# Score matmuls whose contraction rows are packed as 128, 128 and 33, the 33-row ones of two query blocks in different halves of the array

## The chip, the cores and the metric

The kernel runs on one core of one Trainium2 chip. The metric is the time of one execution on the device in microseconds (us), as the median of several runs. Everything read from a trace comes from one profiled execution.

## What is computed

A decoder layer for 16 batches of 100 rows of width 128, with a context of 1444 rows of width 96 a batch. All is float32.

```python
x = x + self_attention(layernorm(x), wq, wk, wv)          # one head, rope, causal
x = x + cross_attention(layernorm(x), ctx, Wq, Wk, Wv, Wo, bo)
x = x + (quantized(layernorm(x)) @ (ternary - 1).T + bias)

# cross_attention: 16 heads of 64
scores = einsum('bqhd,bkhd->bhqk', q, k) / 8              # 16 * 100 queries x 1444 keys a batch
attn = softmax(scores)
out = einsum('bhqk,bkhd->bqhd', attn, v) @ Wo + bo
```

## The kernel before

**Folded weights.** The kernel never forms keys and values by head. At the start it computes, for each head, M = Wq Wk^T (128 x 96) and G = Wv Wo (96 x 128), in *m_bank* and *g_bank*, with 64 contraction rows a head. A batch's queries times M give *q*, 96 rows by 1600 columns (16 heads x 100 queries). The scores are then q against the context itself, transposed (*cT*, 96 rows by keys).

**Split operands.** The matrix unit takes operands rounded to a shorter form (F32R). To keep precision each operand is split into a rounded part and the rest: q_hi and q_lo, cT_hi and cT_lo, and the exponentials pr_hi and pr_lo, the context cN_hi and cN_lo. A product takes three matmuls: hi x hi, hi x lo, lo x hi. For the scores that is 97 + 96 + 96 contraction rows; the 97th is a row of ones in cT_hi and the negated row maximum (*negmax*) in q_hi, so that the maximum is subtracted inside the matmul.

**Steps.** A batch has 24 steps: 2 pairs of query blocks (800 queries each) by 12 chunks of 128 keys. A step's scores are 6 matmuls of 400 columns, three terms by two blocks *a*, each block into its own PSUM bank (*scores*, L1075). ScalarE takes the exponential of both banks twice (L610 in float32, L613 rounded, to *pr* and *pr_hi*), VectorE forms *pr_lo* (L879), and two steps later come the values, 6 matmuls of 400 columns with 128 contraction rows (*values*, L1107, or 2 in L1091 for the last chunk). The output of a pair is copied to *o_sb* (L575).

**Everything else** goes into slots between those matmuls, by a table written by hand (*AT*: step, what, for which batch). The items take turns in two PSUM banks; TensorE's *fill* writes one when VectorE's *consume* has freed it (semaphores misc_ready and misc_free). They are: the self-attention of the batch after next (T1, QK, V, S, PT, AO, T2), the next batch's q (in steps 0, 3, 5 and 8; ScalarE's *high_q*, L568, rounds it, VectorE's L658 forms q_lo), its row maxima (*max*, 39 matmuls of 482 columns in L929, reduced by VectorE in L663, up to four a step), their transpose (*negmax*, step 21), and the rest of the batch before (y, T3, F). In the last batch *sums* (L974, 16 matmul rows of one contraction row each, at partition 96) and *yh* (L979) take the place of *y* (L967). VectorE works its items of a step off, then waits for the exponentials and forms pr_lo.

**POOL** forms cT_lo (L488, L492) and cN_lo (L498) of the next batch and normalizes the output (L505, L506). **The SP queue** issues all DMAs in program order: for a batch the sums of the batch before (move_sums), then, when the splits of the next batch are done (split_done), the context of the batch after it (load_ctx), the store of the batch before, and the negmax row of the next batch (move_negmax: two DMAs from negmaxT into row 96 of q_hi, L391 and L393). The scores of a batch wait for that row and for cT_lo (L1062, L1063). In batch 0 the first part of the row is a DMA of its own (L410). q_hi, q_lo, cT_hi and cT_lo have two buffers each, one for every other batch.

The 12 batches in the middle are a loop of 6 turns with two batches each.

Of the kernel before, what the change touches and what calls it, by code (L numbers as in the profile page):

```python
# [35 lines left out]
def decoder_layer(nc, x_in, ctx_in, ctx_last_in, ctxT_in, wself_in, wqT_in, wkT_in, wvT_in, wo_in, bo_in,  # L36
# [6 lines left out]
    DH, H, _ = wqT_in.shape  # L43
# [25 lines left out]
    LOOPED = B - 4  # L69
    assert STEPS % RING == 0 and STEPS % 2 == 0 and Q % PAIR == 0 and BLK <= 512  # L70
# [3 lines left out]
    with ExitStack() as stack:  # L74
# [14 lines left out]
        wqT = sb("wqT", [DH, H, D])  # L89
        wkT = sb("wkT", [DH, H, DC])  # L90
        wvT = sb("wvT", [DH, H, DC])
        wo = sb("wo", [DH, H, D])
# [34 lines left out]
        o_sb = sb("o_sb", [DC + 1, Q])  # L127
        rrow = sb("rrow", [1, Q])
        rball = sb("rball", [DC, Q])
# [40 lines left out]
        ctx_in_s = sem("ctx_in_s")  # L170
        row_a_in_s = sem("row_a_in_s")
# [182 lines left out]
        def _(sp):  # L354
# [30 lines left out]

            def move_negmax(n, par, use, first=0):


                sp.wait_ge(misc_free, use + 1)
                full = Q // P  # L390
                sp.dma_start(q_hi[par][DC:DC + 1, first * P:full * P].bitcast(F32),  # L391
                             negmaxT[0:full - first, :].bitcast(F32)).then_inc(row_in_s, 16)
                sp.dma_start(q_hi[par][DC:DC + 1, full * P:Q].bitcast(F32),  # L393
                             negmaxT[full - first:QT - first, P - (Q - full * P):P].bitcast(F32)).then_inc(row_in_s, 16)
# [37 lines left out]
        NCONST = 4 + 2 * 6  # L432
# [3 lines left out]
        def _(pool):  # L436
# [19 lines left out]
            def padding(i):  # L456

                constant(cT_hi[i][:, NT:NCH * P], 0.0)
                constant(cT_lo[i][:, NT:NCH * P], 0.0)
                constant(cN_hi[i][:, FULL, :], 0.0)  # L460
                constant(cT_hi[i][DC:DC + 1, 0:NT], 1.0)
# [22 lines left out]
            def split_T(n, par, rows_in=0):  # L484
                pool.wait_ge(cThi_done, 2 * (n + 1))
                at_least(pool, st_ready, (n - 1) * STEPS)
                half = NT // 2
                nc.gpsimd.tensor_tensor(out=cT_lo[par][:, 0:half], in0=cT_raw[:, 0:half],  # L488
                                        in1=cT_hi[par][0:DC, 0:half].bitcast(F32), op=ALU.subtract)

                at_least(pool, rrow_in_s, rows_in * 16)
                nc.gpsimd.tensor_tensor(out=cT_lo[par][:, half:NT], in0=cT_raw[:, half:NT],  # L492
                                        in1=cT_hi[par][0:DC, half:NT].bitcast(F32), op=ALU.subtract).then_inc(cTlo_done, 1)
# [7 lines left out]
            def normalize(n):  # L501
# [3 lines left out]
                order.link(nc.gpsimd.partition_broadcast(rball[:, :], rrow[:, :]))  # L505
                nc.gpsimd.tensor_tensor(out=o_sb[0:DC, :], in0=o_sb[0:DC, :], in1=rball[:, :],  # L506
# [41 lines left out]
        def _(act):  # L548
# [17 lines left out]
            def high_q(n, par, j, use, bank):  # L566
                act.wait_ge(misc_ready, use + 1)
                nc.scalar.activation(q_hi[par][0:DC, j * BLK:(j + 1) * BLK], banks[0:DC, bank, 0:BLK],  # L568
                                     ACT.Copy).then_inc(qhi_done, 1)

            def evacuate(n, pair, y_use=None):
# [3 lines left out]
                nc.scalar.activation(o_sb[:, pair * PAIR:(pair + 1) * PAIR].rearrange("p (a q) -> p a q", a=2),  # L575
# [615 lines left out]
```

## Time and profile before

| what | value |
|---|---|
| median of 3 runs | 1241.41 us (1240.72 to 1242.85) |
| span of the profiled execution | 1241.1 us |
| TensorE matmul rows busy | 1159.2 us, 93% |
| weight loads busy | 1047.9 us, 84% |
| VectorE busy | 1005.4 us, 81% |
| ScalarE busy | 691.1 us, 56% |
| GpSimd (POOL) busy | 245.7 us, 20% |
| mean granted TensorE clock | 0.981 of full |

The profiled execution has a span of 1241.1 us, 0.3 us less than the median of the runs. A batch takes about 74 us, a step about 3.0. Matmuls are pipelined, so the rows of two that follow each other overlap, and a busy share says little of how densely they are issued; the distance between two starts says it. PEld rows are weight loads; each matmul has one.

### The profile page before, as it was taken

What the parts mean: (1) busy time and instruction counts of PE and PEld (TensorE: products, weight loads), DVE (VectorE), ACT (ScalarE), POOL (GpSimd) and SP (SyncE); (2) the same over time, 40 slices, a digit from 0 to 9 for tenths busy, and PEclk for the clock granted to TensorE, in tenths of its full rate; (3) what the DMA queues carried; (4) which work ended last, traced back from release to release, by engine and by line L of the source; (5) the groups of instructions that cost most, each with busy time, mean ns of one, the idle gap of its engine ahead of it and who ended that gap; (6) DMA issues with size and microseconds to landing.
All of it is one profiled execution on the core that took longest, in us unless ns stands there. A gap on an engine that the chain in (4) does not pass through costs nothing.

```text
span 1241.1 us, 20286 instructions
## 1 busy us (share of the span) xinstructions
PE 1159.2 (93%) x6561; PEld 1047.9 (84%) x6561; DVE 1005.4 (81%) x1625; ACT 691.1 (56%) x969; POOL 245.7 (20%) x228
## 2 busy tenths in 40 slices
PE   7789999999999999999999999999999999999997
PEld 5568889898898888888898888989889898988996
DVE  2698888988788798887979878898788889888655
ACT  1245656556464665656556554655556466564653
POOL 3120130302213022130302213130221303022010
PEclk9799999999899999999999999999999999999997
DMA  6101010010101001010000101001010100100000
GB/s 143 38 1 39 1 39 3 6 36 2 39 3 39 4 2 38 4 38 5 16 25 1 39 4 38 3 1 41 3 39 3 39 2 2 40 2 1 3 1 4
DMA packets 12727, 24.40 MB, mean 20 GB/s; under 512 B 4934, under 2 KB 8654, under 8 KB 12494
## 3 DMA queue, kind: packets, MB, share of 16 engines
q1 hardware_dynamic: 12622, 23.00, 6.9%
q8 instruction: 65, 1.06, 0.4%
q14 instruction: 40, 0.33, 0.1%
HBM read 21.88 MB, written 0.82 MB: 18 GB/s over the span
## 4 chain that ended last, share of the span: by engine, by line
PE 77%; issue 10%; DVE 10%; ACT 1%; DMA 1%; DVEq 1%; POOL 0%; SPq 0%; POOLq 0%; ACTq 0%
PE banks L1075 27%; PE banks L1107 26%; PE banks L929 9%; PE banks L967 4%; PE banks L920 4%; DVE pr_lo L879 3%; DVE maxes L663 3%; PE banks L949 1%; DVE cN_hi L775 1%; ACT pr_hi L613 1%; DMA q_hi<-negmaxT 1%; PE banks L1091 1%; PE banks L1010 1%; PE banks L960 1%; PE banks L1038 1%
## 5 line engine op out<-in xcount | busy, mean ns | idle before, releaser
L610 ACT ACTIVATE pr<-banks 128x800 f32<-128x800 f32 x384 | 322.4, 840 | 442.4 <-PE banks L1075 438.3
L879 DVE TENSOR_TENSOR pr_lo<-pr,pr_hi 128x800 fp32r<-128x800 f32 x352 | 424.0, 1205 | 61.2 <-ACT pr_hi L613 54.1
L663 DVE TENSOR_REDUCE maxes<-banks 128x1 f32<-128x482 f32 x585 | 372.5, 653 | 51.0 <-PE banks L929 45.9
L613 ACT ACTIVATE pr_hi<-banks 128x800 fp32r<-128x800 f32 x384 | 319.1, 831 | 0.0
L929 PE MATMUL banks<-cT_hi,q_hi 96*128 96x482 f32 x585 | 228.4, 390 | 27.5 <-DVE maxes L663 18.1
L1075 PE MATMUL banks<-q_hi,cT_hi 97*128 97x400 f32 x768 | 215.6, 362 | 9.1 <-DMA q_hi<-negmaxT 6.9
L1075 PE MATMUL banks<-q_hi,cT_lo 96*128 96x400 f32 x768 | 208.5, 352 | 0.0
L1075 PE MATMUL banks<-q_lo,cT_hi 96*128 96x400 f32 x768 | 203.9, 346 | 0.0
L1107 PE MATMUL banks<-pr_hi,cN_hi 128*97 128x400 f32 x704 | 187.7, 348 | 0.0
L1107 PE MATMUL banks<-pr_lo,cN_hi 128*97 128x400 f32 x704 | 186.9, 347 | 0.6 <-DVE pr_lo L879 0.6
L1107 PE MATMUL banks<-pr_hi,cN_lo 128*96 128x400 f32 x704 | 186.3, 346 | 0.0
L1075 PEld LDWEIGHTS banks<-q_hi,cT_hi 97*128 97x128 f32 x768 | 135.2, 191 | 20.6 <-ACT pr_hi L613 6.4
L929 PEld LDWEIGHTS banks<-cT_hi,q_hi 96*128 96x128 f32 x585 | 109.9, 188 | 50.3 <-DVE maxes L663 26.2
L1075 PEld LDWEIGHTS banks<-q_lo,cT_hi 96*128 96x128 f32 x768 | 143.2, 190 | 0.0
L1075 PEld LDWEIGHTS banks<-q_hi,cT_lo 96*128 96x128 f32 x768 | 139.2, 190 | 3.3
L475 POOL TENSOR_TENSOR ve<-mv,eps 100x1 f32<-100x1 f32 x48 | 9.2, 192 | 616.6 <-DVE mv L642 616.6
L1107 PEld LDWEIGHTS banks<-pr_lo,cN_hi 128*97 128x97 f32 x704 | 115.0, 164 | 16.5 <-DVE pr_lo L879 1.1
L1107 PEld LDWEIGHTS banks<-pr_hi,cN_lo 128*96 128x96 f32 x704 | 114.5, 163 | 15.9
L1107 PEld LDWEIGHTS banks<-pr_hi,cN_hi 128*97 128x97 f32 x704 | 114.3, 164 | 12.5
L506 POOL TENSOR_TENSOR o_sb<-o_sb,rball 96x1600 f32<-96x1600 f32 x15 | 55.6, 3706 | 105.8 <-issue 105.8
L920 PEld LDWEIGHTS banks<-x2T,M 128*96 128x96 f32 x512 | 56.8, 175 | 7.6 <-DVE maxes L663 1.4
L920 PE MATMUL banks<-x2T,M 128*96 128x100 f32 x512 | 59.6, 263 | 2.2 <-DVE maxes L663 1.1
(117 smaller groups left out, 888.3 us busy)
## 6 DMA issues: line engine op xcount, KB each, us to landing
cT_raw<-in_ctxT SPq DMA_DIRECT2D x16, 568.5 KB
cN_raw<-in_ctx SPq DMA_DIRECT2D x16, 528.0 KB
out<-result SPq DMA_DIRECT2D x16, 50.0 KB
X<-in_x SPq DMA_DIRECT2D x1, 700.0 KB
cN_raw<-in_ctx_last SPq DMA_DIRECT2D x16, 40.5 KB
wqT<-in_wqT SPq DMA_DIRECT2D x1, 512.0 KB, 5.4
wo<-in_wo SPq DMA_DIRECT2D x1, 512.0 KB, 13.3
wkT<-in_wkT SPq DMA_DIRECT2D x1, 384.0 KB, 7.0
```

The costliest lines, as they stand in the source:

```text
L506: nc.gpsimd.tensor_tensor(out=o_sb[0:DC, :], in0=o_sb[0:DC, :], in1=rball[:, :], op=ALU.mult).then_inc(on_done, 1)
L610: nc.scalar.activation(pr[:, s % 2, :].rearrange("p (a q) -> p a q", a=2), pair, ACT.Exp, scale=float(DH) ** -0.5).then_inc(exp_done, 1)
L613: nc.scalar.activation(pr_hi[:, s % RING, :].rearrange("p (a q) -> p a q", a=2), pair, ACT.Exp, scale=float(DH) ** -0.5).then_inc(hi_done, 1)
L663: nc.vector.tensor_reduce(maxes[:, t, p:p + 1], here[:, 0:PW], AX.X, ALU.max).then_inc(misc_free, 1)
L775: nc.vector.scalar_tensor_tensor(out=cN_hi[par][0:ROWS, FULL, 0:DC], in0=last_hi[:, :].bitcast(F32), scalar=last[0:ROWS, 0:1], in1=cN_raw[ ...
L879: nc.vector.tensor_tensor(low[rows, s % RING, :], pr[rows, s % 2, :], pr_hi[rows, s % RING, :].bitcast(F32), ALU.subtract).then_inc(lo_don ...
L920: mm = nc.tensor.matmul(here[0:DC, i * S:(i + 1) * S], M[:, h, :], x2T[par][:, :], start=True, stop=True)
L929: mm = nc.tensor.matmul(here[:, 0:PW], q_hi[par][0:DC, qtile(t):qtile(t) + P], cT_hi[par][0:DC, PAT[p]:PAT[p] + PW], start=True, stop=True)
L949: mm = nc.tensor.matmul(here[:, m * S:(m + 1) * S], wself[:, m, :], xnT[par][:, :], start=True, stop=True)
L967: mm = nc.tensor.matmul(here[0:S, 0:D], o_sb[0:DC, h * S:(h + 1) * S], G[:, h, :], start=(h == 0), stop=(h == H - 1))
L1075: mm = nc.tensor.matmul(banks[:, ST + 2 * (s % 2) + a, 0:BLK], k, q[:, q0:q0 + BLK], start=(i == 0), stop=(i == 2))
L1107: mm = nc.tensor.matmul(banks[0:m, OUT + a, 0:BLK], k, e[:, r, a * BLK:(a + 1) * BLK], start=False, stop=(s % NCH == NCH - 1 and i == 2))
```

## The change

The 289 contraction rows of the scores, 97 + 96 + 96, are packed anew, as 128 + 128 + 33:

- a: q_a holds q_hi (96 rows) and q_lo's rows 64 to 95 at partitions 96 to 127; cT_a holds cT_hi (96 rows) and again cT_hi's rows 64 to 95.
- b: q_b holds q_lo's rows 0 to 63 and q_hi's rows 0 to 63; cT_b holds cT_hi's rows 0 to 63 and cT_lo's rows 0 to 63.
- c: q_c holds q_hi's rows 64 to 95 and the negmax row, 33 rows, and the same again at partitions 64 to 96; cT_c holds cT_lo's rows 64 to 95 and the row of ones, also twice.

A step's six score matmuls become two with a, two with b, two with c. The c matmul of block 0 uses partitions 0 to 32, that of block 1 partitions 64 to 96, each into its own bank as before. The number of matmuls, their columns and all sums are the same.

The copies between partitions are made by new DMAs in the SP queue: five for cT (move_c, 224 rows of 1516 words a batch) and three for q (move_q, 128 rows of 1600 words a batch). The negmax row goes out twice, in four DMAs. cT_lo has one buffer now. VectorE forms q_lo in two instructions (32 rows and 64 rows) instead of one. The weights of M and G are stored as 8 heads in partitions 0 to 63 and 8 heads in partitions 64 to 127, and wkT and wvT lie in buffers that are used only later. The maxima (L929) use q_a and cT_a, with 96 rows as before.

```diff
-        q_hi = two("q_hi", [DC + 1, Q], F32R)
-        q_lo = two("q_lo", [DC, Q], F32R)
-        cT_hi = two("cT_hi", [DC + 1, NCH * P], F32R)
-        cT_lo = two("cT_lo", [DC, NCH * P], F32R)
+        q_a = two("q_a", [P, Q], F32R)
+        q_b = two("q_b", [P, Q], F32R)
+        q_c = two("q_c", [HALF + TOP + 1, Q], F32R)
+        cT_a = two("cT_a", [P, NCH * P], F32R)
+        cT_b = two("cT_b", [P, NCH * P], F32R)
+        cT_c = two("cT_c", [HALF + TOP + 1, NCH * P], F32R)
+        cT_lo = sb("cT_lo", [DC, NT], F32R)
...
+            def move_c(n, par):
+
+                sp.wait_ge(cThi_done, 2 * (n + 1))
+                sp.dma_start(cT_a[par][DC:P, 0:NT].bitcast(F32),
+                             cT_a[par][HALF:DC, 0:NT].bitcast(F32)).then_inc(cdup_in_s, 16)
+                sp.dma_start(cT_b[par][0:HALF, 0:NT].bitcast(F32),
+                             cT_a[par][0:HALF, 0:NT].bitcast(F32)).then_inc(cdup_in_s, 16)
+                sp.wait_ge(cTlo_done, n + 1)
+                sp.dma_start(cT_b[par][HALF:P, 0:NT].bitcast(F32), cT_lo[0:HALF, :].bitcast(F32)).then_inc(cdup_in_s, 16)
+                for half in (0, HALF):
+                    sp.dma_start(cT_c[par][half:half + TOP, 0:NT].bitcast(F32),
+                                 cT_lo[HALF:DC, :].bitcast(F32)).then_inc(cdup_in_s, 16)
+
+            def move_q(n, par):
+
+                sp.wait_ge(qhi_done, QB * (n + 1))
+                sp.dma_start(q_b[par][HALF:P, :].bitcast(F32), q_a[par][0:HALF, :].bitcast(F32)).then_inc(qdup_in_s, 16)
+                for half in (0, HALF):
+                    sp.dma_start(q_c[par][half:half + TOP, :].bitcast(F32),
+                                 q_a[par][HALF:DC, :].bitcast(F32)).then_inc(qdup_in_s, 16)
...
+                for row in (TOP, HALF + TOP):
+                    sp.dma_start(q_c[par][row:row + 1, first * P:full * P].bitcast(F32),
+                                 negmaxT[0:full - first, :].bitcast(F32)).then_inc(row_in_s, 16)
+                    sp.dma_start(q_c[par][row:row + 1, full * P:Q].bitcast(F32),
+                                 negmaxT[full - first:QT - first, P - (Q - full * P):P].bitcast(F32)).then_inc(row_in_s, 16)
...
+            move_c(0, 0)
             split_done(0)
             load_ctx(1)
+            move_q(0, 0)
             sp.wait_ge(misc_free, NSTART)
-            sp.dma_start(q_hi[0][DC:DC + 1, 0:FIRST * P].bitcast(F32),
-                         negmaxT[0:FIRST, :].bitcast(F32)).then_inc(row_a_in_s, 16)
+            for row in (TOP, HALF + TOP):
+                sp.dma_start(q_c[0][row:row + 1, 0:FIRST * P].bitcast(F32),
+                             negmaxT[0:FIRST, :].bitcast(F32)).then_inc(row_a_in_s, 16)
...
                     move_sums(b - 1)
+                if present(b, 1):
+                    move_c(b + 1, 1 - par)
                 if present(b, 2):
                     split_done(b + 1)
                     load_ctx(ahead)
+                if present(b, 1):
+                    move_q(b + 1, 1 - par)
...
-                    nc.vector.tensor_tensor(q_lo[par][:, j * BLK:(j + 1) * BLK], here[0:DC, 0:BLK],
-                                            q_hi[par][0:DC, j * BLK:(j + 1) * BLK].bitcast(F32),
-                                            ALU.subtract).then_inc(misc_free, 1)
+                    cols = slice(j * BLK, (j + 1) * BLK)
+                    nc.vector.tensor_tensor(q_a[par][DC:P, cols], here[HALF:DC, 0:BLK],
+                                            q_a[par][HALF:DC, cols].bitcast(F32), ALU.subtract)
+                    nc.vector.tensor_tensor(q_b[par][0:HALF, cols], here[0:HALF, 0:BLK],
+                                            q_a[par][0:HALF, cols].bitcast(F32), ALU.subtract).then_inc(misc_free, 1)
...
-                terms = [(cT_hi[par][0:DC + 1, keys], q_hi[par][0:DC + 1, :]),
-                         (cT_hi[par][0:DC, keys], q_lo[par][:, :]),
-                         (cT_lo[par][:, keys], q_hi[par][0:DC, :])]
-                k, q = terms[i]
                 for a in range(2):
+                    rest = slice(a * HALF, a * HALF + TOP + 1)
+                    terms = [(cT_a[par][:, keys], q_a[par][:, :]), (cT_b[par][:, keys], q_b[par][:, :]),
+                             (cT_c[par][rest, keys], q_c[par][rest, :])]
+                    k, q = terms[i]
                     q0 = pair * PAIR + a * BLK
                     mm = nc.tensor.matmul(banks[:, ST + 2 * (s % 2) + a, 0:BLK], k, q[:, q0:q0 + BLK],
                                           start=(i == 0), stop=(i == 2))
```

Here P is 128, DC 96, HALF 64 and TOP 32. The scores of a batch wait for all copies (cdup_in_s, qdup_in_s) and for the four row DMAs.

## Rows read from the trace of the kernel before

**Rows 1.** The page's header and part 1: busy us (share of span) xinstructions.
```profile
span 1241.1 us, 20286 instructions
...
PE 1159.2 (93%) x6561; PEld 1047.9 (84%) x6561; DVE 1005.4 (81%) x1625; ACT 691.1 (56%) x969; POOL 245.7 (20%) x228
```

**Rows 2.** The page's part 4, the chain that ended last, by engine.
```profile
PE 77%; issue 10%; DVE 10%; ACT 1%; DMA 1%; DVEq 1%; POOL 0%; SPq 0%; POOLq 0%; ACTq 0%
```

**Rows 3.** The same chain in order of time, in the middle: start, us, what.
```profile
570.27 1.10 PE banks L1075 x6
571.36 1.09 PE banks L1107 x6
```

**Rows 4.** Waits of TensorE: line, released by, us in total, times, longest.
```profile
PE banks L929 <- DVE maxes L663: 18.1, 21, 3.1
PE banks L960 <- DVE maxes L663: 15.2, 13, 2.8
...
PE banks L929 <- DVE V L700: 7.5, 14, 0.6
```

**Rows 5.** Timeline, steady stream: start, us, engine, line, operation, rows*columns, moving operand.
```profile
627.33 0.35 PE L1075 MATMUL banks<-q_lo,cT_hi 96*128 96x400 f32 x1
627.33 0.37 PEld L1075 LDWEIGHTS banks<-q_hi,cT_lo 96*128 96x128 f32 x2
```

**Rows 6.** Timeline, last batch, into the one-row matmuls.
```profile
1204.34 0.34 PE L1107 MATMUL banks<-pr_lo,cN_hi 128*97 128x400 f32 x1
1204.61 0.25 PEld L974 LDWEIGHTS banks<-cT_hi,o_sb 1*100 1x100 f32 x2 [0.28 <-issue]
```

**Rows 7.** Timeline, the end, out of the one-row matmuls.
```profile
1228.33 0.22 PE L974 MATMUL banks<-cT_hi,o_sb 1*100 1x1 f32 x1
1228.48 0.54 PEld L979 LDWEIGHTS banks<-G,o_sb 96*100 96x100 f32 x3
```

**Rows 8.** Timeline, the start: out of the 64-row matmuls.
```profile
28.54 0.41 PE L1010 MATMUL banks<-wo,wvT 64*96 64x128 f32 x1
28.88 0.56 PEld L920 LDWEIGHTS banks<-x2T,M 128*96 128x96 f32 x3 [0.28 <-issue]
```

**Rows 9.** Timeline, last batch, the first full-height pair behind the one-row matmuls.
```profile
1206.11 0.30 PEld L1075 LDWEIGHTS banks<-q_hi,cT_hi 97*128 97x128 f32 x2
1206.58 0.35 PE L1075 MATMUL banks<-q_lo,cT_hi 96*128 96x400 f32 x1
```

**Rows 10.** POOL and TensorE near 320; L775 everywhere (ns, min/median/max).
```profile
317.80 3.02 POOL L498 TENSOR_TENSOR cN_lo<-cN_raw,cN_hi 128x1056 fp32r<-128x1056 f32 x1
...
321.55 0.75 PE L960 MATMUL banks<-V,prT 100*100 100x128 f32 x2 [2.82 <-DVE maxes L663]
...
L775 DVE SCALAR_TENSOR_TENSOR cN_hi<-last_hi,last,cN_raw x16: 304/308/2306, 49.5 to 1126.6; 108x96 fp32r<-108x96 f32 x16
```

**Rows 11.** VectorE's groups by shape: xcount, busy us, mean ns, idle before and releaser.
```profile
L879 DVE TENSOR_TENSOR pr_lo<-pr,pr_hi 128x800 fp32r<-128x800 f32 x352 | 424.0, 1205 | 61.2 <-ACT pr_hi L613 54.1 <-issue 3.9 <-ACT pr L610 1.8
L663 DVE TENSOR_REDUCE maxes<-banks 128x1 f32<-128x482 f32 x585 | 372.5, 653 | 51.0 <-PE banks L929 45.9
L658 DVE TENSOR_TENSOR q_lo<-banks,q_hi 96x400 fp32r<-96x400 f32 x64 | 35.1, 548 | 10.6 <-ACT q_hi L568 9.4
```

**Rows 12.** Timeline: the SP queue's last issue and the next batch's first score matmul.
```profile
132.25 0.56 SPq L393 DMA_DIRECT2D q_hi<-negmaxT  x1
...
135.29 0.53 PE L1075 MATMUL banks<-q_hi,cT_hi 97*128 97x400 f32 x2
```

**Rows 13.** SP issues, first scores; a window (last: granted clock, DMA share, GB/s).
```profile
50.75 0.40 SPq L367 DMA_DIRECT2D cN_raw<-in_ctx_last  x1
54.70 0.89 SPq L410 DMA_DIRECT2D q_hi<-negmaxT  x1
...
56.91 0.67 PE L1075 MATMUL banks<-q_hi,cT_hi 97*128 97x400 f32 x1 [2.55 <-DMA q_hi<-negmaxT]
...
321.90:325.30 3.40, 3.40 (x12) 2.95 (x12) 2.82 (x6) 1.56 (x2) 0.00 (x0) 0.50 0.87 245
```

More of the change, by code:

```diff
@@ L69, in decoder_layer @@
     LOOPED = B - 4
+    HALF = P // 2
+    TOP = DC - HALF
+    assert DC + TOP == P and TOP == 32
     assert STEPS % RING == 0 and STEPS % 2 == 0 and Q % PAIR == 0 and BLK <= 512
@@ L567, in high_q @@
                 act.wait_ge(misc_ready, use + 1)
-                nc.scalar.activation(q_hi[par][0:DC, j * BLK:(j + 1) * BLK], banks[0:DC, bank, 0:BLK],
+                nc.scalar.activation(q_a[par][0:DC, j * BLK:(j + 1) * BLK], banks[0:DC, bank, 0:BLK],
                                      ACT.Copy).then_inc(qhi_done, 1)
@@ L928, in fill @@
                         pe.wait_ge(qhi_done, n * QB + bank_of[t] + 1)
-                    mm = nc.tensor.matmul(here[:, 0:PW], q_hi[par][0:DC, qtile(t):qtile(t) + P],
-                                          cT_hi[par][0:DC, PAT[p]:PAT[p] + PW], start=True, stop=True)
+                    mm = nc.tensor.matmul(here[:, 0:PW], q_a[par][0:DC, qtile(t):qtile(t) + P],
+                                          cT_a[par][0:DC, PAT[p]:PAT[p] + PW], start=True, stop=True)
                 elif what == "max_b":
                     t, p = divmod(j, PIECES)
-                    mm = nc.tensor.matmul(here[:, 0:PW], q_hi[par][0:DC, qtile(t):qtile(t) + P],
-                                          cT_hi[par][0:DC, PAT[p]:PAT[p] + PW], start=True, stop=True)
+                    mm = nc.tensor.matmul(here[:, 0:PW], q_a[par][0:DC, qtile(t):qtile(t) + P],
+                                          cT_a[par][0:DC, PAT[p]:PAT[p] + PW], start=True, stop=True)
                 elif what == "negmax_a":
@@ L974, in fill @@
                         mm = nc.tensor.matmul(here[0:S, i:i + 1], o_sb[DC:DC + 1, q0:q0 + S],
-                                              cT_hi[par][DC:DC + 1, 0:1].bitcast(F32), start=True, stop=True)
+                                              cT_c[par][DC:DC + 1, 0:1].bitcast(F32), start=True, stop=True)
                 elif what == "yh":
@@ L996, in start, with head @@
                     fill(n, n, what, 0, k, MISC + k % 2, behind)
+            def head(h):
+                first = h // (H // 2) * DH
+                return slice(first, first + DH), h % (H // 2)
             def m_bank(j):
                 for i in range(4):
-                    mm = nc.tensor.matmul(banks[:, j, i * DC:(i + 1) * DC], wqT[:, 4 * j + i, :],
-                                          wkT[:, 4 * j + i, :], start=True, stop=True)
+                    rows, h = head(4 * j + i)
+                    mm = nc.tensor.matmul(banks[:, j, i * DC:(i + 1) * DC], wqT[rows, h, :], wkT[rows, h, :],
+                                          start=True, stop=True)
                 mm.then_inc(mg_ready, 1)
@@ L1009, in g_bank @@
                 for i in range(4):
-                    mm = nc.tensor.matmul(banks[0:DC, GBANKS[j], i * D:(i + 1) * D], wvT[:, 4 * j + i, :],
-                                          wo[:, 4 * j + i, :], start=True, stop=True)
+                    rows, h = head(4 * j + i)
+                    mm = nc.tensor.matmul(banks[0:DC, GBANKS[j], i * D:(i + 1) * D], wvT[rows, h, :], wo[rows, h, :],
+                                          start=True, stop=True)
                 mm.then_inc(mg_ready, 1)
@@ L1037, in _ @@
                 for p in range(PIECES):
-                    mm = nc.tensor.matmul(banks[:, PIECES * (t % 2) + p, 0:PW], q_hi[0][0:DC, qtile(t):qtile(t) + P],
-                                          cT_hi[0][0:DC, PAT[p]:PAT[p] + PW], start=True, stop=True)
+                    mm = nc.tensor.matmul(banks[:, PIECES * (t % 2) + p, 0:PW], q_a[0][0:DC, qtile(t):qtile(t) + P],
+                                          cT_a[0][0:DC, PAT[p]:PAT[p] + PW], start=True, stop=True)
                 mm.then_inc(max0_ready, 1)
@@ L1167, with halves @@
     cos, sin = np.cos(ang).astype(np.float32), np.sin(ang).astype(np.float32)
+    def halves(w):
+        return w.reshape(DH, 2, H // 2, w.shape[2]).transpose(1, 0, 2, 3).reshape(2 * DH, H // 2, w.shape[2])
     def by_head(w):
-        return np.asarray(w).reshape(w.shape[0], H, DH).transpose(2, 1, 0)
+        return halves(np.asarray(w).reshape(w.shape[0], H, DH).transpose(2, 1, 0))
     named = {
```

62 lines of the change are left out of this document (31 added, 31 removed).

## The prediction

> **What bounds the kernel now.** I read the header and the busy line of the page first [rows 1]. TensorE's matmul rows cover 93% of the span, VectorE 81%, ScalarE 56%. The busy share of TensorE can't be trusted alone, since its rows overlap: one 400-column matmul is shown as 0.35 us long, but its successor starts 0.18 us later. So I went on to the chain that ended last. It lies on TensorE for 77% of the span and on VectorE for 10% [rows 2], and in order of time it reads six score matmuls in 1.10 us, six value matmuls in 1.09 us, again and again [rows 3]. That is 0.183 us for a matmul, whether it contracts 96, 97 or 128 rows. VectorE enters the chain where TensorE has to wait for it: 18.1 us and 7.5 us ahead of the maxima (L929) and 15.2 us ahead of L960, 41 us in these three [rows 4]. What a wait of the queue adds before and after is not in those numbers. So the kernel is bound by the issue of matmuls, with short stops where VectorE has fallen behind: what the change does to the time between two matmuls counts nearly whole, 384 times (16 batches of 24 steps).
>
> **The six score matmuls of a step.** Their number stays six: two of 128 rows, two of 128 rows, and two of 33, at partitions 0 and 64. Rows cost nothing, as said, so the first four keep 4 x 0.183 us. All that can change is the last pair. Two things may happen to it: the two may run at the same time, and the array may have to be regrouped from 128 rows to halves of 64 and back, since everything before and behind the pair uses more than 64 rows.
>
> The trace of before has such regroupings, outside the steady loop, and they are not free. In the steady stream the weights of the next matmul load as soon as the running one starts: the matmul starts at 627.33, and so does the load of the next one, 627.33 [rows 5]. In the last batch the "sums" matmuls contract one row, at partition 96. The last full-height matmul before them starts at 1204.34, is 0.34 long, and the first weight load of the one-row group comes at 1204.61, 0.27 us after that start instead of 0.00 [rows 6]. That load waited for nothing that the profile shows ("issue"). The way back is the same: the last one-row matmul starts at 1228.33, is 0.22 long, and the load of the 96-row one comes at 1228.48 [rows 7]. In both the load begins 0.07 us before the shown end of the last matmul of the other height: it waits until the array has run empty. With 64-row matmuls it is seen too, at the start of the kernel, where all matmuls take longer: the last one starts at 28.54, the load of the 128-row one behind it at 28.88 [rows 8]. Between 96, 97 and 128 rows there is no such gap: the two lines follow each other at 0.183 [rows 3].
>
> Behind each gap the weights are no longer hidden. After the gap the load starts at 1206.11; the two matmuls of its pair are followed by the next line at 1206.58, so the first of them really began at 1206.58 - 2 x 0.183 = 1206.21, 0.10 us after its load. The second load of the pair starts 0.30 - 0.19 = 0.11 us after the first [rows 9].
>
> So a step goes like this, from the start of the last 128-row score matmul: 0.27 until the first 33-row load, 0.11 until the second, 0.10 until the second 33-row matmul runs (the first has started 0.11 earlier and they overlap), 0.27 until the load of the next full-height one, 0.10 until that runs: 0.85 us. Before it was 3 x 0.183 = 0.55 us. That is +0.30 us a step, 384 x 0.30 = +115 us.
>
> The bounds of this: if the second 33-row matmul doesn't overlap the first but follows at 0.183, the step costs 0.075 more, 384 x 0.375 = +144 us. If nothing is drained and the two overlap fully but for the second load (0.11 + 0.11 - 0.183, so 0.03 late), the pair takes one matmul's time: -0.15, and 384 x -0.15 = -58 us. The row nearest to the case is the one of the kernel itself at full clock, the drain, and I take +0.30 for it; that two halves overlap is shown by no row here, and I take it because the weight loads of one group already overlap a running matmul.
>
> The Trainium skill, "TensorEngine Tiling (Array Packing)", Key Properties, says that a change of the tiling mode, not just of the tile, drains TensorE. By that rule the sum is the one above, and the rows agree with it: 0.27 us in place of 0.00. The skill's "TensorE: Matmul & The Clock Gate", Part 3, gives the span of packed tiles as one matmul and some 4 ns for each further tile; alone it would give the -58 us, or 384 x -0.18 = -69 us. It speaks of a stream that stays packed, and here two of twelve matmuls are.
>
> **What VectorE gives back.** TensorE stands still for 41 us behind VectorE [rows 4], and every such stop also leaves the next weights unhidden, 0.1 us for each of the 48 in these three rows, 5 us. VectorE's work, 1005 us, doesn't shrink; a step of TensorE that is 0.3 us longer lets it catch up. One step with three maxima costs VectorE 1.2 + 3 x 0.65 = 3.2 us [rows 11] and TensorE 12 x 0.183 for the 400 columns and 3 x 0.183 x 482 / 400 for the maxima, 2.9 us, with the change 3.2. So most of these stops go. I take 40 us back of the 46 (bounds 15 and 60, below). Some batches have a worse stop: POOL's L498, 3.02 us long, runs when VectorE comes to L775, which takes up to 2.31 us where 0.31 is its median, and TensorE stops for 2.8 us [rows 10]. Right behind it the granted clock is 0.50, the 1.2 GHz level, for all of a window of 3.4 us [rows 13], which costs about half of that again, 1.7 us. Longer steps move POOL and VectorE against each other. If no batch meets it any more, the clock comes back too, and 60 us return; if many do, only 15.
>
> **Smaller terms.** *q_lo* is now written in two pieces. One piece of 96 rows and 400 columns takes 0.55 us [rows 11]. If the time goes with the columns, the second piece costs that again, 64 x 0.55 = 35 us of VectorE's own time; if it went with the rows, nothing. Both pieces have the 400 columns, so I take the 35. It has the room (1040 of over 1300 us), but in the steps 0, 3, 5 and 8 it holds back maxima behind it: I charge 6 us, between 0 and 35.
>
> The *maxima row* goes out in four DMAs instead of two. The SP queue issues the last of the two at 132.25; the first matmul that needs it is at 135.29 [rows 12], and TensorE doesn't wait there. The landing time is known from the start: issued at 54.70, waited for until 56.91 [rows 13], so 2.2 us. The slack is 135.29 - 132.25 - 2.2 = 0.8 us, and the last of four is issued two issues later, 0.56 + 0.89 = 1.4 us; but two longer steps lie between, +0.6. So 0.0 us a batch in my case, 1.4 + 0.3 - 0.8 = 0.9 where steps get shorter (15 batches, 14 us).
>
> The *copies* of move_c (224 rows of 1516 words, 1.36 MB) and of move_q (128 rows of 1600, 0.82 MB) stand in the same SP queue. In a batch they have tens of us. At the start they don't: move_q is queued behind load_ctx(1), whose 1.14 MB (568.5, 528.0 and 40.5 KB) are issued up to 51.15, and the first scores, at 56.91, come to wait for both [rows 13]. At the 245 GB/s of the stretch with the densest transfers, loads and copies take 1.96 MB / 245 GB/s = 8.0 us; from 50 on, with the 2.2 us until something lands, that is some 60.5, so +4 us, with the rows of the maxima behind it in the queue (bounds 0 and 8). In batch 0 the second part of the maxima row is 1.4 us later too; its cover is unknown, +1. POOL's two more memsets for each buffer stand ahead of nothing that is late. The weights M and G are computed by the same number of matmuls from halves of 64 rows that all lie in one half per bank: nothing.
>
> **Sum.** 1241.1 (span of the profiled execution; with 0.3 around it the median of the runs, 1241.4) + 115 + 6 + 0 + 4 + 1 - 40 = 1327, and 0.3 around it: **1328 us**.
>
> **The rivals.**
> *A (forecast, 0.72)*: drained twice a step. Own range: with 60 us given back 1308, and with the 6 and 5 us of small terms hidden as well 1297; high with no overlap of the halves (+29) at 1357: 1296 to 1357.
> *B, drained once a step (0.10)*: only the regrouping into halves waits, and the full-height load behind the pair is started as usual. 0.27 + 0.11 + 0.10 + 0.18 = 0.66 against 0.55: 384 x 0.11 = +42 us, + 11 small terms, - 20 given back: 1274. For it: a load into other rows might be allowed. Against it: the ways back [rows 7, 8].
> *C, the other side (0.11)*: no drain, the halves run together. -58, + 5 at the start, + 14 for the maxima row, + 6, and 15 more of waits for VectorE, whose 3.2 us in a step with three maxima are then the longer: 1223. For it: the rows that show a drain are few, and all of them are of operands declared F32, where the scores have F32R ones. Against it: in [rows 6] the matmul before the gap is an F32R one, and F32 matmuls of 96 rows follow F32R ones without a gap. It decides from the point where a regrouping costs less than half of the 0.15 us won, 0.075; the rows show 0.19 (0.27 + 0.10 - 0.18).
> *D, the change does nothing (0.07)*: neither drained nor overlapped, the pair takes 2 x 0.183 as ever. What is left are the small terms, 1241 + 11 = 1252, to 1246 if the start is covered.
>
> **How the numbers follow.** The predicted time is A's. The range leaves out C and the tails: 1246 to 1357 holds about 0.67 of A, all of B, and most of D, some 0.8. Faster by over 0.2% (about what a measurement of this kernel can tell from no change) is C: 0.11. Within 0.2% is the lower edge of D: 0.02. Slower is the rest, 0.87.
>
> **What would show it.** In the profile after: each step has two gaps in the weight loads, 0.27 us after the last 128-row score matmul and 0.27 us after the second 33-row one; the two 33-row matmuls start about 0.11 us apart; six scores and the way back take 1.40 us in place of 1.10. The waits of L929 and L960 for VectorE are a third of what they were. The first scores start near 60 or 61 us. If the loads of the 33-row pair stand directly at the start of the matmul before them, C or D is right, and the distance between the two 33-row matmuls tells which. I'd be wrong with the right mechanism if the halves don't overlap, or if POOL and VectorE now collide in many batches.

## The result: slower by 3.8%

The changed kernel takes 1289.39 us (median of 4, 1286.28 to 1291.63) where the kernel before, on the same chip, takes 1241.58 (median of 4, 1240.72 to 1242.85). The ratio is 1.0376, with a 95% interval of 1.035 to 1.0403: 48 us more. The forecast was 1328, +87, with 1246 to 1357 as its range. So the side was right and the mechanism too, as the following shows, but the forecast change was nearly double the measured one.

The page of the profiled execution after (1286.3 us, span 1284.5), the lines that answer to [rows 1] and [rows 2], and the two groups of the new 33-row matmuls:

```profile
span 1284.5 us, 20543 instructions
...
PE 1226.5 (95%) x6561; PEld 955.0 (74%) x6561; DVE 1022.2 (80%) x1689; ACT 692.0 (54%) x969; POOL 245.6 (19%) x232
...
PE 81%; DVE 9%; issue 7%; ACT 1%; DMA 1%; DVEq 1%; POOL 0%; SPq 0%; POOLq 0%; ACTq 0%
...
L1123 PE MATMUL banks<-q_c,cT_c 33*128 33x400 f32 x768 | 173.3, 447 | 0.0
...
L1123 PEld LDWEIGHTS banks<-q_c,cT_c 33*128 33x128 f32 x768 | 71.8, 184 | 98.3 <-issue 93.1
```

The same 6561 matmuls fill 67 us more, and the weight loads 93 us less than in [rows 1]: two loads of each step now lie over each other, which is 384 x 0.19 = 73 of the 93. The last number pair of the last row is what to see: the load engine was idle for 98.3 us ahead of the 33-row loads, 93.1 of it with nothing that the profile shows as a reason. Spread over 384 steps that is 0.26 us a step, the 0.27 of [rows 6].

One step on TensorE in the timeline after, in the middle of the kernel, answering to [rows 3] and [rows 5]:

```profile
632.44 0.53 PE L1123 MATMUL banks<-q_b,cT_b 128*128 128x400 f32 x2
632.90 0.19 PEld L1123 LDWEIGHTS banks<-q_c,cT_c 33*128 33x128 f32 x2 [0.26 <-issue]
632.90 0.45 PE L1123 MATMUL banks<-q_c,cT_c 33*128 33x400 f32 x2
633.28 0.19 PEld L969 LDWEIGHTS banks<-cT_a,q_a 96*128 96x128 f32 x1 [0.19 <-issue]
633.28 0.48 PE L969 MATMUL banks<-cT_a,q_a 96*128 96x482 f32 x1
633.60 0.34 PE L1155 MATMUL banks<-pr_hi,cN_hi 128*97 128x400 f32 x1
```

The second b matmul starts at 632.44 + 0.18 = 632.62. The 33-row loads come 0.28 us after it. A row with x2 covers both instructions: the two loads take 0.19 us together, where [rows 9] had 0.30 for a pair, and the two matmuls 0.45, as long as one of them alone (mean 447 ns above). So both start at the same time: over all 384 pairs the second starts 0.002 to 0.004 us after the first, loads and matmuls alike. The next full-height load comes 0.38 us after them. The value matmul at 633.60 is behind the maxima's 482 columns, 0.22 us, so the maxima really began at 633.38. From the last full-height start to the next it is 0.76 us, where three matmuls took 0.55: +0.21 us a step, and 384 x 0.21 = 81 us.

TensorE's waits after (line, released by, us in total, times, longest), answering to [rows 4]:

```profile
PE banks L969 <- DVE maxes L703: 13.3, 17, 1.7
PE banks L969 <- DVE q_b L699: 6.2, 8, 1.1
...
PE banks L1123 <- DMA q_c<-q_a: 5.8, 1, 5.8
...
PE banks L1000 <- DVE maxes L703: 2.1, 6, 0.7
PE banks L1123 <- DMA q_c<-negmaxT: 1.9, 2, 1.0
```

L969 and L1000 are the lines L929 and L960 of before. The two waits for maxima, 18.1 and 15.2 us, have become 13.3 and 2.1, and the wait for V has gone from 7.5 to 0.6. The wait for q_b, 6.2, was one of 1.6 for q_lo before. Together that is 42.4 before and 22.2 after. The rows of the maxima are waited for 1.9 us in all, in spite of the four DMAs. The 5.8 us are the start:

```profile
60.42 1.01 PE L1123 MATMUL banks<-q_a,cT_a 128*128 128x400 f32 x2 [5.79 <-DMA q_c<-q_a]
...
65.00:70.00 5.00, 4.69 (x13) 3.09 (x13) 4.21 (x8) 2.06 (x3) 3.65 (x4) 0.50 0.00 0
70.00:75.00 5.00, 5.00 (x15) 3.80 (x14) 3.79 (x7) 1.56 (x2) 0.62 (x1) 0.50 0.00 0
```

The first scores start 3.5 us later than in [rows 13], and the granted clock stays at 0.50, the 1.2 GHz level, until 75.0. In the kernel before it is back at 61.2, 13.8 us earlier, and the window that follows has 1.00:

```profile
65.00:70.00 5.00, 2.89 (x17) 2.39 (x15) 4.99 (x7) 1.56 (x2) 2.15 (x2) 1.00 0.00 0
```

Over the whole kernel the mean clock is the same, 0.981 before and 0.982 after: what is lost at the start, before loses in later stretches (17 us at the 1.2 GHz level between 300 and 1200, where the changed kernel has none). The first exponential of batch 1 and that of batch 15 give the time of a batch between them, after and (second fence) before:

```profile
145.18 0.84 ACT L648 ACTIVATE pr<-banks 128x800 f32<-128x800 f32 x1 [0.98 <-PE banks L1123]
1204.48 0.84 ACT L648 ACTIVATE pr<-banks 128x800 f32<-128x800 f32 x1 [0.81 <-PE banks L1123]
```

```profile
136.67 0.84 ACT L610 ACTIVATE pr<-banks 128x800 f32<-128x800 f32 x1 [0.70 <-PE banks L1075]
1164.84 0.84 ACT L610 ACTIVATE pr<-banks 128x800 f32<-128x800 f32 x1 [0.62 <-PE banks L1075]
```

That is (1204.48 - 145.18) / 14 = 75.66 us a batch against 73.44: +2.2, where 24 steps of +0.21 would make +5.0. More than half of what the regrouping costs does not reach the end of a batch. Two questions stood, then: is the regrouping really the cause, and where does the other half go?

### The profile page after: what moved, and what is told of

Same layout as the page of the kernel before. It is cut to its first block, busy times and chain, and to the rows that moved or that the text cites. A ratio compares the mean times of both kernels' runs of the same rounds, so it can differ in the third digit from the quotient of the medians.

```text
span 1284.5 us, 20543 instructions
## 1 busy us (share of the span) xinstructions
PE 1226.5 (95%) x6561; PEld 955.0 (74%) x6561; DVE 1022.2 (80%) x1689; ACT 692.0 (54%) x969; POOL 245.6 (19%) x232
## 3 DMA queue, kind: packets, MB, share of 16 engines
q1 hardware_dynamic: 21454, 57.96, 18.1%
## 4 chain that ended last, share of the span: by engine, by line
PE 81%; DVE 9%; issue 7%; ACT 1%; DMA 1%; DVEq 1%; POOL 0%; SPq 0%; POOLq 0%; ACTq 0%
PE banks L1123 28%; PE banks L1155 28%; PE banks L969 12%; PE banks L1007 4%; PE banks L960 3%; DVE pr_lo L919 2%; DVE maxes L703 2%; PE banks L1139 1%; DVE q_a L697 1%; DVE q_b L699 1%; PE banks L989 1%; DMA q_c<-q_a 1%; PE banks L1000 1%; PE banks L1046 0%; DVE maxes L859 0%
## 5 line engine op out<-in xcount | busy, mean ns | idle before, releaser
L919 DVE TENSOR_TENSOR pr_lo<-pr,pr_hi 128x800 fp32r<-128x800 f32 x352 | 391.1, 1111 | 69.1 <-ACT pr_hi L651 64.8
L969 PE MATMUL banks<-cT_a,q_a 96*128 96x482 f32 x585 | 247.6, 423 | 20.4 <-DVE maxes L703 13.3
L1123 PE MATMUL banks<-q_a,cT_a 128*128 128x400 f32 x768 | 217.2, 364 | 9.2 <-DMA q_c<-q_a 5.8
L1123 PE MATMUL banks<-q_b,cT_b 128*128 128x400 f32 x768 | 203.7, 346 | 0.0
L1123 PE MATMUL banks<-q_c,cT_c 33*128 33x400 f32 x768 | 173.3, 447 | 0.0
L969 PEld LDWEIGHTS banks<-cT_a,q_a 96*128 96x128 f32 x585 | 109.8, 188 | 76.5 <-issue 28.0
L1123 PEld LDWEIGHTS banks<-q_a,cT_a 128*128 128x128 f32 x768 | 135.1, 192 | 22.8 <-issue 7.9
L1123 PEld LDWEIGHTS banks<-q_c,cT_c 33*128 33x128 f32 x768 | 71.8, 184 | 98.3 <-issue 93.1
L1123 PEld LDWEIGHTS banks<-q_b,cT_b 128*128 128x128 f32 x768 | 143.2, 189 | 0.0
L606 ACT ACTIVATE q_a<-banks 96x400 fp32r<-96x400 f32 x64 | 32.0, 501 | 60.9 <-PE banks L960 60.9
L960 PEld LDWEIGHTS banks<-x2T,M 128*96 128x96 f32 x512 | 55.8, 171 | 6.4 <-DVE maxes L703 1.2
```

The lines of the kernel that those rows point to most:

```text
L606: nc.scalar.activation(q_a[par][0:DC, j * BLK:(j + 1) * BLK], banks[0:DC, bank, 0:BLK], ACT.Copy).then_inc(qhi_done, 1)
L919: nc.vector.tensor_tensor(low[rows, s % RING, :], pr[rows, s % 2, :], pr_hi[rows, s % RING, :].bitcast(F32), ALU.subtract).then_inc(lo_don ...
L960: mm = nc.tensor.matmul(here[0:DC, i * S:(i + 1) * S], M[:, h, :], x2T[par][:, :], start=True, stop=True)
L969: mm = nc.tensor.matmul(here[:, 0:PW], q_a[par][0:DC, qtile(t):qtile(t) + P], cT_a[par][0:DC, PAT[p]:PAT[p] + PW], start=True, stop=True)
L1123: mm = nc.tensor.matmul(banks[:, ST + 2 * (s % 2) + a, 0:BLK], k, q[:, q0:q0 + BLK], start=(i == 0), stop=(i == 2))
```

## Experiments

All medians are in microseconds, and ratios are to the kernel before on the same chip (1241.1 to 1241.4 there).

**1. The 33-row matmuls at full height.** Everything of the change stays, but the c matmuls contract 97 rows (partitions 0 to 96, the unused ones zero), so that nothing is regrouped and nothing runs side by side. One copy to cT_c falls away with it.

```diff
-                    rest = slice(a * HALF, a * HALF + TOP + 1)
+                    rest = slice(0, HALF + TOP + 1)
```

> The changed kernel, but the c matmuls of both blocks are of full height (97 rows, partitions 0 to 96, the unused ones zero), so nothing is regrouped and nothing can overlap; copies, rows, q_lo in two pieces stay (one copy of eight is gone). Theory (the two regroupings of a step cost 0.42 us less the 0.21 that the overlap wins, 384 x 0.21 = 81 us, of which VectorE's waits had given back some 45): the step's scores take 1.10 us again, the waits for VectorE come back, and the time is near that of before plus the start, 1250 us (1244 to 1260). Rival (the time went to the new copies, the row DMAs and the second q_lo piece): it stays at 1285 to 1290.

1250.78 (1248.57 to 1255.13), ratio 1.0061 (1.0033 to 1.009). The six scores are back at 1.09 us, in the chain in order of time:

```profile
642.12 1.09 PE banks L1121 x6
```

So 38.6 of the 48 us come with the height of two matmuls in twelve, and 9.6 with everything else: the copies, the start and q_lo's two pieces. The chain says that a step lost its 0.21 us, 81 us in all; only 38.6 of them came off the time. A part of the others turned up as waits (L967 is L929 of before, L998 is L960):

```profile
PE banks L967 <- DVE maxes L701: 21.2, 20, 2.6
PE banks L998 <- DVE maxes L701: 8.7, 13, 0.7
PE banks L1121 <- DMA q_c<-negmaxT: 8.5, 12, 1.4
```

**2. Both 33-row matmuls in the same half.** Two regroupings a step as in the changed kernel, and no overlap.

```diff
-                    rest = slice(a * HALF, a * HALF + TOP + 1)
+                    rest = slice(0, TOP + 1)
```

> The changed kernel, but both 33-row matmuls use partitions 0 to 32, so they can't run at the same time; the regroupings stay. Theory: the second follows the first at 0.18 us instead of 0.003, 384 x 0.18 = +69 us, little of it given back since VectorE's stops are mostly gone: 1340 to 1360. Rival (the shown overlap is only in the records, the matmuls take turns anyway): no change, 1289.

1335.8 (1335.08 to 1341.19), ratio 1.0753 (1.0722 to 1.0784). The pair in the timeline:

```profile
641.43 0.29 PEld L1123 LDWEIGHTS banks<-q_c,cT_c 33*128 33x128 f32 x2
...
641.43 0.63 PE L1123 MATMUL banks<-q_c,cT_c 33*128 33x400 f32 x2
```

Now the pair of loads takes 0.29 and the pair of matmuls 0.63, instead of 0.19 and 0.45: in one half the second load comes 0.11 us after the first and the second matmul 0.18 behind. The overlap of the halves is real and worth 0.18 us a step, 69 us on TensorE, of which 46 show in the time. That is a little more given back than expected: 1335.8 lies under the 1340 to 1360. The prediction had charged the 0.11 us between the loads to the changed kernel. There they don't exist; they appear only here, in one half, and even here they cost nothing of their own: from the pair's loads to the next full-height load it is 0.56 us, the changed kernel's 0.38 and the second matmul's 0.18.

**3. One matmul more in each step of the kernel before.** The step gets longer by 0.183 us without any regrouping (the added product, cT_lo by q_lo for block 0, is also added to the scores).

```diff
+                if i == 1:
+                    q0 = pair * PAIR
+                    nc.tensor.matmul(banks[:, ST + 2 * (s % 2), 0:BLK], cT_lo[par][:, keys], q_lo[par][:, q0:q0 + BLK],
+                                     start=False, stop=False)
```

> The kernel before with one more matmul of 400 columns a step (the product of both low parts, added for block 0 alone): TensorE gets 384 x 0.183 = 70 us more work of a known size and nothing else changes. Theory (each 0.2 us that a step gets longer gives half of it back, since POOL's and VectorE's stops get out of the way): 1265 to 1290, and VectorE's long waits for POOL get fewer as in the changed kernel. Rival (what was given back came from something else in the change, the longer step counts whole): 1305 to 1312.

1281.63 (1277.01 to 1285.92), ratio 1.0307 (1.0271 to 1.0343): 40 of 384 x 0.183 = 70 us reach the end, 57%. Batches take 75.84 us. So time that is added to TensorE's step without any change of height is about half absorbed too. Waits are part of where it goes:

```profile
PE banks L929 <- DVE maxes L663: 14.5, 17, 1.9
PE banks L960 <- DVE maxes L663: 7.3, 13, 2.3
```

The other half of the expectation failed: VectorE's long pr_lo instructions did not get fewer (68 of over 1.2 us here, 64 in before), though in the changed kernel there are 39.

**4. The copies ahead of the next batch's context at the start.**

```diff
             move_c(0, 0)
+            move_q(0, 0)
             split_done(0)
             load_ctx(1)
-            move_q(0, 0)
```

> The changed kernel with batch 0's move_q ahead of split_done and load_ctx(1) in the SP queue. Theory (the first scores wait 5.8 us for the copies queued behind 1.14 MB, and that pause keeps the granted clock at half for 13.7 us longer, 6.8 us of work): first scores near 57, clock back at full near 60 us after the start of the records' pause, 1277 to 1282. Rival (the clock's return isn't tied to that pause): only the 3.5 us of the wait, 1285 to 1287.

1285.76 (1285.21 to 1289.41), ratio 1.0359 (1.0325 to 1.0394). That is the rival's time and not the theory's; it is 3.6 us under the changed kernel, and the ranges of the two overlap. The first scores come 2.2 us earlier, and the clock returns only 2 us earlier, at 72.9:

```profile
58.19 1.01 PE L1123 MATMUL banks<-q_a,cT_a 128*128 128x400 f32 x2 [3.25 <-issue]
...
70.00:75.00 5.00, 5.00 (x19) 3.91 (x20) 3.47 (x7) 3.02 (x4) 0.00 (x0) 0.71 0.00 0
```

The pause before the first scores became shorter by 2.5 us only, so this run doesn't separate it. Up to 90 us, the stretches at 0.50 are 44.2 to 61.2 in the kernel before; 41.8 to 65.7 and 69.1 to 72.5 in experiment 1, which has the long pause and no regrouping; 42.2 to 72.9 here; 44.3 to 75.0 in the changed kernel; 42.4 to 83.4 in experiment 2, whose regroupings have no overlap. With regroupings the clock returns later. But experiment 6, which has none, is at 0.50 from 42.3 to 66.2 and from 69.6 to 76.4, together as long as the changed kernel (30.7 us). So what keeps the clock low at the start stays open.

**5. q_lo in two pieces in the kernel before.** VectorE forms rows 64 to 95 and 0 to 63 by themselves, as the changed kernel does.

```diff
-                    nc.vector.tensor_tensor(q_lo[par][:, j * BLK:(j + 1) * BLK], here[0:DC, 0:BLK],
...
+                    nc.vector.tensor_tensor(q_lo[par][64:DC, cols], here[64:DC, 0:BLK],
...
+                    nc.vector.tensor_tensor(q_lo[par][0:64, cols], here[0:64, 0:BLK],
```

> The kernel before with q_lo formed in two VectorE instructions (rows 64 to 95 and rows 0 to 63) and nothing else. Theory (a part of the 9.7 us by which e1_full_height is over the kernel before is this second piece, 64 x 0.57 = 36 us of VectorE's time, hidden but for some holding back of maxima): VectorE's busy time up by 36, the run 2 to 8 us over before, 1243 to 1249. Rival (all of the 9.7 us is the start and its clock): 1241.

1243.65 (1241.79 to 1246.49), ratio 1.0011 (0.999 to 1.0033), not to be told from before. VectorE's own time rises by 21 us, not by 36. The two pieces take 37.8 us more than the one, but pr_lo gets shorter by 28.6 us and cN_hi (L775, [rows 10]) by 6.0, while *qk*, a sum in the self-attention that reads two tensors of SBUF, gets longer by 18.1 (first row: before; the others: this run):

```profile
L698 DVE TENSOR_TENSOR qk<-rt 128x200 f32<-128x200 f32 x16 | 5.9, 368 | 1.6
...
L881 DVE TENSOR_TENSOR pr_lo<-pr,pr_hi 128x800 fp32r<-128x800 f32 x352 | 395.4, 1123 | 60.2 <-ACT pr_hi L613 53.1 <-issue 2.8 <-ACT pr L610 1.8
...
L700 DVE TENSOR_TENSOR qk<-rt 128x200 f32<-128x200 f32 x16 | 24.0, 1501 | 1.6
```

pr_lo takes 1123 ns in the mean against 1205 [rows 11] and 1202 in experiment 3, where the steps are longer and q_lo is in one piece. Experiment 1, with two pieces and steps of the old length, has 1138, the changed kernel 1111. In these traces, one of each kernel, the shorter pr_lo thus goes with the two pieces of q_lo, which move VectorE against POOL, and not, as the forecast had it, with the longer steps. Nor does VectorE simply meet POOL less: qk takes 1.4 us in the changed kernel too, where it took 0.37 before. A part of the collisions has only moved to it.

**6. Five full-height matmuls a step.** Experiment 1 without the b matmul of block 1, which leaves that product out of the scores. A step then has the time that the packing would have if nothing were drained.

```diff
+                    if (i, a) == (1, 1):
+                        continue
```

> e1_full_height with the b matmul of block 1 left out (small parts of the product, not the maximum's row), so five full-height matmuls a step: TensorE's time as if the pair really cost one matmul and nothing were regrouped. Theory (per 0.18 us of a step about half reaches the end, from e3_one_more: 70 us more gave 40): 1250.8 - 35 = 1216, 1208 to 1228. Rival (VectorE and POOL hold the steps where they are once TensorE is faster): over 1235. Rival (TensorE bound alone, all of it counts): 1180.

1221.11 (1220.01 to 1226.03), ratio 0.9848 (0.9815 to 0.988): 30 us under experiment 1, of 70 taken off. TensorE now waits more, for VectorE and for the rows of the maxima:

```profile
PE banks L967 <- DVE maxes L701: 28.3, 28, 2.5
PE banks L967 <- DVE q_b L697: 15.8, 42, 1.0
PE banks L1123 <- DMA q_c<-negmaxT: 13.0, 9, 2.2
```

This is rival C, the undrained packing, as nearly as it can be run (it takes 70 us off TensorE where C had 58), and its 1223 was close.

**7. POOL's long instructions in pieces, in the kernel before.** The product of 1600 columns in four of 400, the forming of cN_lo in three.

```diff
-                nc.gpsimd.tensor_tensor(out=o_sb[0:DC, :], in0=o_sb[0:DC, :], in1=rball[:, :],
-                                        op=ALU.mult).then_inc(on_done, 1)
+                for k in range(4):
+                    cols = slice(k * BLK, (k + 1) * BLK)
+                    part = nc.gpsimd.tensor_tensor(out=o_sb[0:DC, cols], in0=o_sb[0:DC, cols], in1=rball[0:DC, cols],
+                                                   op=ALU.mult)
+                part.then_inc(on_done, 1)
```

> The kernel before with POOL's product for the output cut into 4 pieces of 400 columns and cN_lo into 3. Theory (VectorE's pr_lo, two inputs in SBUF, stands until the running POOL instruction ends, 65 times, 77 us in all, and that is what a longer step gave back): a stand ends after a piece, at most 1 us, TensorE's waits for VectorE get shorter, 1215 to 1232. Rival (POOL's next piece goes ahead of the waiting VectorE instruction, or pieces only make POOL longer): 1241 or over.

1218.7 (1218.06 to 1219.65), ratio 0.9819 (0.9795 to 0.9843), faster than both kernels. In the timeline of before, a pr_lo that begins while a POOL TENSOR_TENSOR runs ends 0.85 us after that one does, in all 67 cases of the trace. One of them:

```profile
609.89 3.64 POOL L506 TENSOR_TENSOR o_sb<-o_sb,rball 96x1600 f32<-96x1600 f32 x1 [7.04 <-issue]
...
611.58 2.80 DVE L879 TENSOR_TENSOR pr_lo<-pr,pr_hi 128x800 fp32r<-128x800 f32 x1
```

POOL ends at 613.53, VectorE at 614.38, and 0.98 us is what the instruction takes alone; it stood for 1.8 us. The pieces, 1.1 and 1.4 us long here, give it a chance sooner:

```profile
601.84 1.23 DVE L884 TENSOR_TENSOR pr_lo<-pr,pr_hi 128x800 fp32r<-128x800 f32 x1
...
602.18 3.34 POOL L499 TENSOR_TENSOR cN_lo<-cN_raw,cN_hi 128x384 fp32r<-128x384 f32 x3
```

The wait that answers to L960 fell from 15.2 to 2.3 us. The clock is a part of the gain. Its mean over the run is 0.983 in before (median of 13 runs) and 0.990 here (median of 4), so before spends some 2 x 0.017 x 1241 = 42 us at the lower level and this kernel 2 x 0.0105 x 1219 = 26, and the difference is worth up to half of these 16 us, 8 of the 23. In the profiled executions the 17 us at 0.50 between 300 and 1200 are gone.

**8. The same pieces in the changed kernel**, on top of experiment 4.

```diff
-                nc.gpsimd.tensor_tensor(out=cN_lo[par][:, :, :], in0=cN_raw[:, 0:FULL, :],
...
+                for first, end in ((0, 4), (4, 8), (8, FULL)):
+                    part = nc.gpsimd.tensor_tensor(out=cN_lo[par][:, first:end, :], in0=cN_raw[:, first:end, :],
```

> e4_copies_first with the same POOL pieces. Theory: the changed kernel has less of these stands (41 us), so it wins less than the kernel before, 5 to 15 us: 1271 to 1281. Rival: as much as the kernel before wins, the regroupings and the stands are independent.

1280.14 (1279.51 to 1281.71), ratio 1.0309 (1.0284 to 1.0334): 5.6 us under experiment 4. The same cure gives 23 us in the kernel before and 5.6 here. One reason is that there is less to take: VectorE's busy time falls by 16.6 us in experiment 7 (1005.4 to 988.8) and by 8.1 here (1025.0 to 1016.9). That the longer steps had absorbed the rest already is argued and not shown.

**9. Finer pieces in the kernel before**, eight of 200 columns and five of two or three chunks.

```diff
-                for k in range(4):
-                    cols = slice(k * BLK, (k + 1) * BLK)
+                for k in range(8):
+                    cols = slice(k * BLK // 2, (k + 1) * BLK // 2)
```

> e7_pool_pieces with finer pieces: the output's product in 8 of 200 columns, cN_lo in 5. Theory (a stand lasts until the running piece ends): a little more, 1212 to 1218. Rival (each POOL instruction costs a start of its own, and the split is done later): 1219 to 1226.

1215.52 (1214.81 to 1216.08), ratio 0.9795 (0.9752 to 0.9837). This is the best version: 26 us under the kernel before and 74 under the changed one.

**10. The two 33-row matmuls apart.** In the changed kernel, block 0 takes a, c, b and block 1 a, b, c, so that each 33-row matmul stands alone between full-height ones.

```diff
-                    k, q = terms[i]
+                    turn = ((0, 2, 1), (0, 1, 2))[a][i]
+                    k, q = terms[turn]
```

> The changed kernel with the two 33-row matmuls of a step taken apart: order a, a, c of block 0, b, b, c of block 1. Same matmuls, four regroupings a step instead of two, and no overlap. Theory (a regrouping makes the next matmul start 0.37 us after the last one instead of 0.18): a step's six take 4 x 0.37 + 2 x 0.18 = 1.85 us instead of 1.30, 384 x 0.55 = +211 us, of which two thirds to nearly all reach the end (e2_same_half: 46 of 70): 1425 to 1495. Rival (a regrouping is dear only because the two loads of the pair come at once, alone it is half that): 1340 to 1380.

1499.27 (1493.11 to 1512.34), ratio 1.21 (1.2012 to 1.2187). Here the pattern of the regrouping stands twice in a step:

```profile
702.80 0.44 PE L1124 MATMUL banks<-q_c,cT_c 33*128 33x400 f32 x1
703.17 0.63 PE L1124 MATMUL banks<-q_b,cT_b 128*128 128x400 f32 x2
703.73 0.45 PE L1124 MATMUL banks<-q_c,cT_c 33*128 33x400 f32 x1
704.11 0.61 PE L1156 MATMUL banks<-pr_hi,cN_hi 128*97 128x400 f32 x2
```

Every change of height costs 0.37 us from load to load, where 0.18 is a matmul's share: 0.19 each. Two more of them and the overlap lost make 2 x 0.19 + 0.18 = 0.56 us a step, 384 x 0.56 = 215, and the time rose by 210 over the changed kernel, 4 us above the expected range. But the steps alone don't make these 210. Between 100 and 670 us the granted clock of this trace is at 0.50 for 44.5 us, in five stretches, where the changed kernel has none; that costs up to 22 us. The longest, from 651.9 to 665.6, comes right behind a stop of TensorE of 2.77 us for VectorE. The batches without such a stretch take 86.9 us (median) against 75.8 in the changed kernel: 11.1 of the 24 x 0.56 = 13.4 reach the end, 83%. So less is absorbed once TensorE's steps are that much longer than VectorE's, but not nothing.

## Why the prediction came out as it did

**The mechanism: right.** The array is drained on the way into the halves and on the way back, in every step, and both drains had the size read from a few rows at the end of the kernel: 0.27 forecast and 0.28 measured on the way in, and on the way back 0.38 from the pair's loads to the next one, where 0.10 + 0.27 was forecast. The Trainium skill's "TensorEngine Tiling (Array Packing)", Key Properties, with its drain at a change of mode, agrees with these rows. The Trainium skill's "TensorE: Matmul & The Clock Gate", Part 3, with its some 4 ns for a further tile, agrees with the pair itself, whose second matmul starts 2 to 4 ns after the first here. But the saving that follows from it alone, 69 us, is 0.18 us a step, and the two changes of height around it cost 0.39 by these rows.

**The term that was mis-sized: "0.11 until the second".** The sum of a step was 0.27 + 0.11 + 0.10 + 0.27 + 0.10 = 0.85, with the 0.11 taken from a pair of full-height loads [rows 9]. The two loads into different halves started within 0.004 us of each other; only in the same-half run are they 0.11 apart. Without it the sum is 0.74, and 0.76 was measured: +0.21 a step in place of +0.30, 81 us in place of 115. The term alone is 42 us too much, the rest of the sum 8 too little, and the 34 that remain are nearly the whole miss of 39. They were enough to put 1289.4 below the forecast's own range, 1296 to 1357. It lies in the stated range only because that reaches down to 1246 for the sake of B and D, so that it holds the measured time is luck as far as A's terms go.

**The small terms: right in sum, in part by luck.** Start 4, q_lo 6, batch 0 another 1: 11 us forecast, 9.6 measured by experiment 1 (which has one copy less). The start itself was 3.5 of 4. The second q_lo piece costs its columns (574 and 567 ns a piece, 548 for the one piece of before), some 36 us of VectorE, but in the kernel before it makes 2.4 us that can't be told from nothing, where 6 were charged. What makes up the rest of the 9.6 was not taken apart. The row DMAs were hidden, as forecast: 1.9 us of wait, where the same DMAs are waited for 8.5 us in experiment 1 with its shorter steps.

**What VectorE gives back: right in size, half right in cause.** 81 + 9.6 - 47.8 = 43 us came back, 40 were forecast. The waits of L929 and L960 for VectorE were to fall to a third and fell to half, 42.4 us to 22.2. Experiment 1 waits 40.4 us for VectorE (21.2, 8.7, 8.1 for q_b and 2.4 for V) and 8.5 for the rows of the maxima, in 59 waits; the changed kernel waits 22.2 and 1.9, in 36. That is 25 us, and with 0.1 us for the unhidden load of each of the 23 waits that are gone it is 27 of the 43. The other 16 I could not place, and that the 40 came out so near is in part luck. POOL holds pr_lo up less often, but that goes with the two pieces of q_lo, and qk is held up instead. The worst stop, L775 behind POOL's L498, is gone in every batch (cN_hi takes 0.31 us in the mean), and so are the low stretches in the middle; but the clock gave nothing in sum, since it returned 13.8 us later at the start, which the forecast did not have.

**The rivals.** B, one drain, gave 1274, nearer to the measured time than the forecast, but by accident: both drains are in the rows. C fell on its own condition: a change of height costs 0.19, over its 0.075. D fell with the timeline, which shows both the drains and the overlap.

Shown: the two drains, the overlap, that the second load of the pair costs nothing, and that TensorE time added or removed near the time of before counts about half (40 of 70, 38.6 of 81, 46 of 69, 30 of 70), and more of it, 83%, once the steps are 0.56 us longer still. Only argued: that this half is VectorE's reserve and nothing else.

## What to carry to other kernels

Before packing small contractions side by side, count the changes of tile height: here each costs 0.19 us and a pair run side by side returns 0.18, so by this estimate a packed stretch must hold three pairs or more between two changes (no run here has more than one), and one pair in each step loses. A per-step price must then go through the waits that the longer step hides: put one harmless extra matmul into each step and measure what share of it reaches the end. And when TensorE waits for VectorE, look at what POOL is running at that moment; cutting POOL's instructions took 26 us off the kernel before, and the time of an ideal packing 20.

## What the runs showed of the hardware that was not expected

- Weight loads into different halves of the rows start together: two took 0.19 us in all here, 0.29 in the same half.
- A VectorE instruction that reads two tensors of SBUF stands until the running POOL instruction has ended (2.80 us instead of 0.98), while the maxima, read from PSUM, keep their 0.65 beside it. The Trainium skill's "GPSIMD Engine Reference", section 1, Specifications, says that POOL shares its SBUF interfaces with VectorE, with contention when a VectorE instruction has two inputs in SBUF, and this trace agrees.
- With regroupings in batch 0 the granted clock came back to 1.0 at 75.0 and, without the overlap, at 83.4, against 61.2 and 65.7 without them; but several kernels without them (experiments 1, 3, 5 and 6) fell to 0.50 once more right after. What holds it low, no run here separates.
